# An edge MLP moved whole ahead of the first convolution, channel by channel, in a graph kernel on one NeuronCore

## The reference, cut to what matters

```python
x = hood_coords                                    # edge_attr_3, 25000 x 3
d = gelu(layer_norm(x @ Wd1 + bd1, g1, b1))        # -> 25000 x 64
d = gelu(layer_norm(d @ Wd2 + bd2, g2, b2))        # -> 25000 x 64
...
logits = w1[target] - w2[source] + d
...
out = segment_sum(a * (w3[source] + d), target)
```

## Time and profile before

| what | value |
|---|---|
| device time, 3 runs | 2391.5, 2373.78, 2384.97 us; median 2384.97 |
| span of the profiled execution, first to last instruction | 1831.4 us |
| mean granted PE clock over the span | 0.951 |
| busy, share of the span: PE, DVE, POOL, ACT | 83%, 81%, 67%, 40% |
| layer 1 of the MLP (34.4 to 99.2) | 64.8 us, granted clock 0.51 |
| roots and layer 2, 19 chunks (99.2 to 140.7) | 41.5 us |
| conv 1 (140.7 to 682) and conv 2 (710.7 to 1266) | 541 and 555 us |
| layer 2, 6 chunks, between the convolutions | ends at 710.68 us |
| last pass of the MLP (1268 to 1295.2) | 27 us |

### The profile page before, as it was taken

How to read it: one execution, slowest core, us unless ns; L and a number is a source line. 1 busy time by engine, 2 the same in 40 slices (tenths; PEclk the granted TensorE clock), 3 DMA queues, 4 the chain that set the end, 5 groups by cost and what they waited for, 6 DMA issues and landing times.

```text
span 1831.4 us, 33936 instructions
## 1 busy us (share of the span) xinstructions
PE 1524.8 (83%) x7745; PEld 989.1 (54%) x7745; DVE 1481.5 (81%) x2831; ACT 732.2 (40%) x1841; POOL 1228.0 (67%) x1207
## 2 busy tenths in 40 slices
PE   2977888888888986999999999997777767667764
PEld 1264566566656665777777777775443334334432
DVE  3688999999999985999999999986777667666664
ACT  2463333333333323323322333223655545554553
POOL 4004777777777757777777777751577777777776
PEclk8588999999999997999999999998999999998998
DMA  5993444444444534887777777773233332333230
GB/s 99 164 110 65 101 104 107 100 106 101 106 105 101 106 73 124 242 233 231 228 225 221 227 227 226 233 221 88 60 80 67 80 67 68 69 77 69 67 73 19
DMA packets 408085, 232.10 MB, mean 127 GB/s; under 512 B 305989, under 2 KB 381958, under 8 KB 408046
## 3 DMA queue, kind: packets, MB, share of 16 engines
q1 hardware_dynamic: 311730, 151.97, 31.2%
q0 software_dynamic: 44864, 65.52, 16.4%
q10 hardware_dynamic: 51452, 14.18, 6.1%
HBM read 141.71 MB, written 92.64 MB: 128 GB/s over the span
## 4 chain that ended last, share of the span: by engine, by line
PE 34%; POOL 11%; issue 8%; DVE 3%; DMA 3%; ACT 3%; POOLq 0%; DVEq 0%; ACTq 0%; SPq 0%
PE bank L980 17%; POOL gath L581 6%; POOL out_dram L588 6%; PE bank L973 3%; PE bank L1039 2%; PE bank L1022 2%; DMA gath<-M,gidx 2%; PE bank L1101 2%; PE bank L1011 2%; PE bank L1031 1%; PE bank L1000 1%; PE bank L1048 1%; DMA arena<-T 1%; PE bank L1120 1%; DVE arena L1570 1%
## 5 line engine op out<-in xcount | busy, mean ns | idle before, releaser
L980 PE MATMUL bank<-Wk,arena 128*128 128x320 f32 (+1 forms) x2352 | 657.6, 465 | 56.9 <-ACT arena L762 56.9
L980 PEld LDWEIGHTS bank<-Wk,arena 128*128 128x128 f32 (+1 forms) x2352 | 328.0, 189 | 304.6 <-issue 223.3
L581 POOL DMA_INDIRECT gath<-T,gidx x392 | 387.1, 988 | 146.9 <-issue 111.1
L581 POOL DMA_INDIRECT gath<-in_x_dram,gidx x196 | 197.3, 1007 | 161.1 <-ACT gidx L679 102.3
L581 POOL DMA_INDIRECT gath<-M,gidx x196 | 213.5, 1089 | 124.9 <-issue 55.8
L762 ACT ACTIVATE arena<-bank 128x256 f32<-128x256 f32 (+1 forms) x392 | 169.6, 433 | 308.3 <-PE bank L973 307.8
L588 POOL DMA_INDIRECT T<-srow,sidx x196 | 214.6, 1095 | 79.4 <-issue 66.8
L1348 DVE TENSOR_TENSOR arena<-bank,A 128x320 f32<-128x320 f32 x392 | 191.6, 489 | 66.4 <-PE bank L980 59.2
L588 POOL DMA_INDIRECT out_dram<-srow,sidx x196 | 199.8, 1019 | 61.3 <-issue 60.7
L973 PE MATMUL bank<-ident,arena 128*128 128x128 f32 x980 | 171.7, 274 | 10.6 <-DVE arena L1328 10.5
L973 PEld LDWEIGHTS bank<-ident,arena 128*128 128x128 f32 x980 | 124.6, 142 | 41.5 <-issue 7.3
(11 more groups left out here) (185 smaller groups left out, 2738.8 us busy)
## 6 DMA issues: line engine op xcount, KB each, us to landing
arena<-T SPq DMA_DIRECT2D x48, 816.0 KB
T<-arena SPq DMA_DIRECT2D x96, 272.0 KB
T<-zero ACTq DMA_DIRECT2D x1, 13281.2 KB, 103.9
B<-arena SPq DMA_DIRECT2D x49, 256.0 KB
arena<-B SPq DMA_DIRECT2D x49, 256.0 KB, 3.8
arena<-in_x_dram SPq DMA_DIRECT2D x48, 256.0 KB, 4.1
out_dram<-arena SPq DMA_DIRECT2D x48, 256.0 KB, 3.5
begins_cut<-begins_d SPq DMA_DIRECT2D x49, 128.5 KB, 3.5
```

The source lines that it names most:

```text
L581: pool.indirect_dma_start(out=gath[slot][:, j, k, 0:width], out_offset=None, in_=table, in_offset=bass.IndirectOffsetOnAxis(gidx[slot][:, ...
L980: return pe.matmul(bank[2 + r][:, 0:KO], ZT[q][rows, chunk, :], Wk[n - 1][rows, weights].rearrange("p k o -> p (k o)"), start=start, stop= ...
```

## The change

What it does, stage by stage:

- **Row loads.** Each piece of 67 partitions becomes one of 64 and one of 3 (`SPANS1`), each 68-partition store of the restart rows one of 64 and one of 4. The loads are 25 instead of 19, the stores 7 instead of 5. The piece of 127 partitions (`rows_i[1:P, 2]`) stays.
- **Variance of layer 1 before layer 1.** With centred weights the variance of `x @ Wd1 + bd1` is a quadratic form in (x, 1) with the 4 x 4 matrix of channel means of weight products. Three small PE operations and DVE copies make the matrix (`gram`), twelve DVE operations of 128 x 200 the form, ACT the root, DVE the reciprocal, and `E3x` is scaled by it once (128 x 800). Before this ACT makes all spline weights.
- **Inputs turned at once.** 25 transposes of 128 x 32 into seven banks; ACT and DVE copy them into one `e3T` of 25 blocks.
- **One loop for both layers** (`m1`). For each chunk PE makes layer 1 with the weights of `Wd1` stationary (4 matmuls of 32 rows x 128 columns), so channels lie on the partitions at once; ACT applies Gelu straight from PSUM; PE makes layer 2 (one matmul, 512 columns); DVE adds the bias into `DT`; ACT squares; PE sums the squares over the partitions with 4 matmuls whose weights are the squares and whose streaming operand `halves` has 2 columns.
- **Last pass ahead of conv 1** (`m2`). Root and reciprocal for all; for each chunk POOL spreads the reciprocals to 128 x 512 (`rstd_rows`), PE turns them, DVE multiplies `DT` by them, ACT applies the second Gelu in place.
- **Gone** are the 6 chunks between the convolutions and the pass after conv 2.

```diff
+    SPANS1 = ((0, FULL1 // 16 * 16), (FULL1 // 16 * 16, FULL1))
...
-                sp.dma_start(rows_i[0:FULL1, q, P:2 * P],
-                             v[P * P:P * P + FULL1 * P].rearrange("(t p) -> t p", p=P)).then_inc(s_rows, 16)
+                for lo, hi in SPANS1:
+                    sp.dma_start(rows_i[lo:hi, q, P:2 * P],
+                                 v[(P + lo) * P:(P + hi) * P].rearrange("(t p) -> t p", p=P)).then_inc(s_rows, 16)
...
@@ @block.gpsimd @@
-            each(pool, step, 3, 1, ahead=3)
+            for g in (-3, -2):
+                step(Group(None, g))
+
+            def spread_rstd(g):
+                wait(pool, m2["turn"], g - 2)
+                pool.tensor_copy(rstd_rows[g.parity], mst[:, 1, bass.ds(g.times(MT), MT)].unsqueeze(2)
+                                 .broadcast_to([P, MT, C])).then_inc(m2["spread"].sem, 1)
+
+            pool.wait_ge(s_rstd, 3)
+            each(pool, spread_rstd, 0, 0, MG)
+            each(pool, step, 1, 1, ahead=3)
...
@@ @block.scalar @@
+            hat_weights()
+            act.wait_ge(s_quad, QUAD)
+            act.activation(mst[:, 1, :], mst[:, 0, :], ACT.Sqrt, bias=eps_col[:, :]).then_inc(s_root, 1)
...
             def step(g):
...
+                    wait(act, m1["layer1"], e)
+                    wait(act, m1["layer2"], e - 2)
+                    act.activation(mg[e.parity], bank[e.parity][:, :], ACT.Gelu, scale=mcol["g1"][:, :],
+                                   bias=mcol["b1"][:, :]).then_inc(m1["gelu"].sem, 1)
...
+                    act.activation(mq[g.parity][:, :, :].rearrange("p t c -> p (t c)"), chunk_of_DT(g), ACT.Square)\
...
+            each(act, step, 1, 0, MG)
+            end_of(act, m1["var"], MG)
+            act.activation(mst[:, 0, :], bank[7][:, 0:MG * MT], ACT.Sqrt, bias=eps_col[:, :]).then_inc(s_root, 1)
...
+            def step(g):
+                wait(act, m2["norm"], g)
+                act.activation(chunk_of_DT(g), chunk_of_DT(g), ACT.Gelu,
+                               scale=mcol["g2"][:, :], bias=mcol["b2"][:, :]).then_inc(m2["gelu"].sem, 1)
+
+            each(act, step, 0, 0, MG)
...
@@ @block.tensor @@
+            pe.wait_ge(s_mw, MLP_WEIGHTS)
+            pe.matmul(bank[6][:, 0:1], centre[:, :], mcol["bd2"][:, :], start=True, stop=True).then_inc(s_gram, 1)
...
+            pe.wait_ge(s_rstd, 2)
+            for e in range(MG):
+                tr = pe.transpose(bank[e // 4][0:4 * MT, e % 4 * P:e % 4 * P + P],
+                                  E3x[:, e * MT:e * MT + MT, :].rearrange("p t c -> p (t c)"), ident[:, :])
...
             def step(g):
...
+                    wait(pe, m1["gelu"], e - 2)
+                    for q in range(PAIRS):
+                        mm = pe.matmul(bank[e.parity][:, q * P:q * P + P],
+                                       Wd1[:, 2 * q:2 * q + 2, :].rearrange("k t c -> k (t c)"),
+                                       e3T[:, bass.ds(e.times(1), 1), :].rearrange("k t e -> k (t e)"),
+                                       start=True, stop=True)
...
+                    wait(pe, m1["gelu"], g)
                     wait(pe, m1["keep"], g - 2)
+                    pe.matmul(bank[2 + g.parity][:, :], Wd2[:, :, :].rearrange("k t c -> k (t c)"), mg[g.parity],
+                              start=True, stop=True).then_inc(m1["layer2"].sem, 1)
+                if (g - 1).within(MG):
+                    e = g - 1
+                    wait(pe, m1["square"], e)
+                    for q in range(PAIRS):
+                        mm = pe.matmul(bank[7][:, bass.ds(e.times(MT, 2 * q), 2)],
+                                       mq[e.parity][:, 2 * q:2 * q + 2, :].rearrange("p t c -> p (t c)"),
+                                       halves[:, :], start=True, stop=True)
...
@@ @block.vector @@
             def step(g):
...
+                wait(dve, m1["layer2"], g)
+                V_.tensor_scalar(chunk_of_DT(g), bank[2 + g.parity][:, :], bd2[:, :], None, ALU.add)\
+                    .then_inc(m1["keep"].sem, 1)
...
+            each(dve, step, 0, 0, MG)
+            dve.wait_ge(s_root, 2)
+            V_.reciprocal(mst[:, 1, :], mst[:, 0, :]).then_inc(s_rstd, 1)
+            end_of(dve, m1["keep"], MG)
...
+                wait(dve, m2["turn"], g)
+                V_.tensor_tensor(chunk_of_DT(g), chunk_of_DT(g), bank[g.parity][:, :], ALU.mult)\
+                    .then_inc(m2["norm"].sem, 1)
```

More of the change, by code:

```diff
@@ L279, in build @@
         XT = [att_mem.take([P, EG]) for _ in (0, 1)]
-        mx3 = [att_mem.take([P, MT * C]) for _ in (0, 1)]
         rec.append(att_mem.take([P, TPG, C]))
@@ L930, in step @@
-                    pe.matmul(bank[2 + g.parity][:, :], e3T[g.parity], Wd1[:, :, :].rearrange("k t c -> k (t c)"),
-                              start=True, stop=True).then_inc(m1["product"].sem, 1)
-            each(pe, step, 1, 0, MG)
-            def turn_chunk(g, s, mx):
-                wait(pe, s["norm"], g)
-                wait(pe, s["gelu"], g - 2)
-                for q in range(MT // 2):
-                    tr = pe.transpose(bank[g.parity][:, q * P:q * P + P], mx[g.parity][:, q * P:q * P + P],
-                                      ident[:, :])
-                tr.then_inc(s["turn"].sem, 1)
@@ L945, in layer2 @@
-            def layer2(first, last):
-                def step(g):
-                    if (g + 1).within(last, first):
-                        turn_chunk(g + 1, m2, mx)
-                    if g.within(last, first):
-                        wait(pe, m2["gelu"], g)
-                        wait(pe, m2["keep"], g - 2)
-                        for q in range(MT // 2):
-                            mm = pe.matmul(bank[2 + g.parity][:, q * P:q * P + P], mg[g.parity][:, q * P:q * P + P],
-                                           Wd2[:, :, :].rearrange("k t c -> k (t c)"), start=True, stop=True)
-                        mm.then_inc(m2["product"].sem, 1)
-                each(pe, step, 1, 0, last, first=first)
@@ new lines, in _, with step @@
+            each(pe, step, 1, 1, MG)
+            def step(g):
+                wait(pe, m2["norm"], g - 2)
+                wait(pe, m2["spread"], g)
+                for q in range(PAIRS):
+                    tr = pe.transpose(bank[g.parity][:, q * P:q * P + P],
+                                      rstd_rows[g.parity][:, 2 * q:2 * q + 2, :].rearrange("p t c -> p (t c)"),
+                                      ident[:, :])
+                tr.then_inc(m2["turn"].sem, 1)
+            each(pe, step, 0, 0, MG)
@@ new lines, in _, with of @@
+            dve.wait_ge(s_gram, 2)
+            part(V_.tensor_copy(bd2[:, :], bank[6][:, 0:1]))
+            dve.wait_ge(s_gram, 3)
+            part(V_.tensor_copy(gram[:, :, :].rearrange("p a b -> p (a b)"), bank[7][:, 16:32]))
+            parts_done()
+            part(V_.tensor_scalar(gram2[:, :, :], gram[:, :, :], 2.0, None, ALU.mult))
+            parts_done()
+            def of(t, i, j):
+                return t[:, i, j:j + 1]
+            comp = [E3x[:, :, c] for c in range(3)]
+            form = [mst[:, k, :] for k in range(3)]
@@ new lines, in _ @@
+            for k in range(3):
+                part(V_.tensor_scalar(form[k], comp[k], of(gram, k, k), of(gram2, k, 3), ALU.mult, ALU.add))
+            parts_done()
+            for k, j in ((0, 1), (1, 2)):
+                part(V_.scalar_tensor_tensor(out=form[k], in0=comp[j], scalar=of(gram2, k, j), in1=form[k],
+                                             op0=ALU.mult, op1=ALU.add))
+            part(V_.tensor_tensor(form[2], form[2], comp[2], ALU.mult))
+            parts_done()
+            part(V_.scalar_tensor_tensor(out=form[0], in0=comp[2], scalar=of(gram2, 0, 2), in1=form[0],
+                                         op0=ALU.mult, op1=ALU.add))
@@ L1256, in set_up @@
+            def set_up():
+                dve.wait_ge(s_rst, RESTARTS)
                 for i in (0, 1):
```

272 lines of the change are left out of this document (131 added, 141 removed).

## The result

The kernel before took 2393.74 us (median of 20 runs, 2368.22 to 2430.83), the changed kernel 2418.4 (20 runs, 2397.12 to 2448.76): 24.7 us or 1.0% between the medians. The ratio, from the runs that the chip did not disturb, is 1.0183 with a 95% interval of [1.0149, 1.0217]; a second set on one chip gave 1.0132 [1.0077, 1.0187]. By the ratios the change makes the kernel 1.3 to 1.8% slower, by the medians of all runs 1.0% and, in the second set, 0.6%. I had forecast 2453 in a range of 2374 to 2474, so the sign and the range were right and the size was too large.

The account below looks back on a forecast made before the run. It took one chain until conv 1 and POOL's pace in attention to bound the kernel. Terms +79.6, -0.3 and -11.5 summed to +67.8 on 2384.97, giving 2453 us; range for 8 in 10: 2374 to 2474.

Parts of the forecast that it names:

- Row loads: At the kernel's start: rows complete near 10.5 us (10 to 17), some 14 earlier, not gained because ACT's queue is next.
- Start of the loop: Chain ahead of the merged MLP loop: it starts at 38.8 us against 34.4 before, +4.4.
- The level: PE's granted clock in the MLP loop: low, 1.2 GHz, so 25 chunks take 151 us; chance 0.58.
- The chunk: PE's time per MLP loop chunk: 2.08 + 2.07 + 1.9 = 6.05 us at low clock, 3.2 at high.
- Last pass: MLP's final pass ahead of conv 1: 1.0 us per chunk, paced by POOL's copy; DVE enters conv 1 at 220.
- I take the 553.6 us between span and median to stay.: Whole kernel: the change alters the span of 1831.4 us, while the 553.6 us beyond it remain.
- PE about 90% busy: In the convolutions: PE is busy about 90% of the time, and the change does not touch them.
- rival 1: MLP loop: the high clock holds throughout, 3.2 us per chunk, -2.7 us in all, 2382 us; chance 0.27.
- Between the convolutions: Removing six MLP chunks there: DVE starts some 3 us earlier but waits for the next gather, -0.3 us.
- After conv 2: Removing the MLP pass there: attention starts 12.3 us earlier, less 0.8 for slow first PE products, -11.5.
- rival 2: MLP loop: the clock changes on the way, about half of the 70 us difference, 2418 us; chance 0.10.
- Rival 4: MLP's last pass: POOL's copy costs 2.0 us per chunk, 25 us more, 2478 with low clock; chance 0.06.

Follow-up runs that it names:

- e2: Changed kernel with layer 1 on all 128 rows of the array, zeros in the added weight rows; 0.986 [0.9803, 0.9918] of the kernel before.
- e3: Changed kernel with one weight load and one 8-column product per chunk for the variance instead of four each; 4.23 us per chunk, no run time given.
- c1_before: The kernel before with no edit, profiled afresh beside the others; its span is 2428.6 us.
- e1: The kernel before with only the new row loads and restart stores; 2484 us (4 runs) beside 2429 of before.
- e4: The kernel before with only the new row loads and restart stores, run once more; 2375.88 us (4 runs) beside 2380.34 of before.
- e6: The kernel before, with GpSimd's first gathers of conv 2 waiting until the six MLP chunks are done; 1.003 [0.9971, 1.0089] of before.

## Why the prediction was right, and where its size was off

The place-by-place sum: entry 59.5 later than in the fresh profile of before, gap 1 11.4 shorter, gap 2 23.3 shorter, together +24.8 us, uncertain by some 10 for the scatter of the gaps. The forecast had +79.6, -0.3 and -11.5, together +67.8. Point by point:

**Row loads.** Forecast 10.5 (10 to 17), measured 14.27: SyncE's last row load was issued by 10.52, where I had 7. That a piece of 67 rows passes row after row is in the traces: in the kernel before SyncE's queue moved 24 packets in the 2 us from 7.5 to 9.5, with a piece of 67 in it, and 131 in the half us from 3.0 with one of 128; from 9 to 12 it moved 36, and 332 in the changed kernel. The difference hid behind ScalarE's queue as forecast: its hat weights began at 22.73 (21.6).

**Start of the loop.** 38.8 forecast, 39.41 measured: right, each step of that chain within 1.1 us.

**The level.** Low, as forecast, and e2 (1.0) and e3 (0.50) show the reason given: the 32-row products. Right, for the largest term.

**The chunk.** 6.05 forecast, 5.51 measured. Mis-sized term: weight loads with two-column products are 1.71, not 1.9, and the next matmuls start 0.35 before the ones ahead have ended. 25 x 0.54 = 13.5 us. The 3.2 for the high level has 0.1 in it that no run shows: in e2 TensorE is busy for 10.00 of 10.00 us from 50 to 60, and the chunk is 1.14 + 1.02 + 0.95 less 0.46 of overlap, 2.65. The third part, 0.95, had been put at 1.0.

**Last pass.** 1.0 forecast, measured 0.81 per chunk (200.59 - 180.37 over 25 chunks, with GpSimd's copy at 0.61, though VectorE was busy beside it for 16.25 of the 19.50 us from 181 to 200.5, and ScalarE's Gelu at about 0.8): 5 us. With the chunk that makes the entry 200.6 instead of 220.

**"I take the 553.6 us between span and median to stay."** This step failed. They were not outside the span: c1_before has 1.7 us there. They lie in the convolutions and the attention stage, as late handovers from TensorE and, with them, a lower granted clock; how they divide between the two is not shown. Therefore both prices that I read from the shown execution for the MLP's work behind the convolutions were too low.

**Readings.** "PE about 90% busy" holds for conv 1 of the execution shown ahead (469 of 531 us), not for conv 2, where TensorE was busy for 541.6 of 543. And "layer 1 had no pauses either", said against rival 1, is too strong: rows 1 leave TensorE idle for 7.3 of 64.8 us. The changed kernel's loop, idle for 1.07 us and low all the same, is what bears the argument out.

**Between the convolutions.** Forecast -0.3, measured -11.4. Beside GpSimd's burst the six chunks took 42 us, not the 14 of the execution shown ahead. What took their place is the same burst beside conv 2's first group (in the changed kernel VectorE waited 17.2 us for one product there, to 949.66). That not all of the 28 us came back fits this; no run separates it.

**After conv 2.** Forecast -11.5, measured -23.3. The 25 chunks took 27.2 us in the execution shown ahead and some 39 in the fresh one.

So the forecast erred by 20 us in the entry and by 23 in the gaps, both to the same side. What the medians and the ratio show, +15 to +44, has the sum of +25 within it, but the ratio's intervals (18 to 52 us) lie mostly above it; whether the convolutions add 10 us in the changed kernel stays open, since conv 1 alone differs by 19 us between the two profiles of the changed kernel and by 109 between e1 and e4, which are the same code.

Rival 1 (high level, no change in time) did not happen, but e2 shows what it is worth: entry at 133.6, where it had 149.8. What decided the level was the number of rows. That the median of 2418 is also the figure of rival 2 is chance: rival 2 put half of the chunks at the high level, and the loop of the changed kernel was at 0.50 from 60 us on. The figure was reached from 2453 by a cheaper chunk and by gaps that were worth more. Rival 4 (dear copies) fell with 0.61 us per copy.

## What to carry to other kernels

Before moving a stage, ask at which granted clock it runs and why: the whole MLP ahead of conv 1 was a loss of 1.3 to 1.8% with layer 1 on 32 rows of the array and a gain of 1.2 to 1.4% with zeros added to fill 128, with the same result and fewer microseconds per product. The same zeros in the kernel before, with the new row loads, gave as much without moving the MLP. And hold the span of a trace against the time of a run: where they differ by hundreds of us, the missing time may lie inside the program, and prices from that trace are then too low exactly beside the work that it shows undisturbed. Here the MLP's work behind conv 1 took 42 us beside GpSimd's indirect DMAs and 15 without them; but taking it away from them (e6) gained nothing by itself, since the burst then delayed the next step.
